# Eight steps of attention ahead of the mask flag instead of six, a set-up in another order with multiplied constants, and the mask words split between two engines, in a fused attention and expert kernel on one Trainium2 core

## The chip, the cores and the metric

The kernel runs on one core of one Trainium2 chip. The metric is the device time of one execution in microseconds. All times inside the execution are counted from the start of the profile's span.

## What is computed

The reference is one block of a network on 2048 rows of 256 numbers: gated cross attention on a context of 1601 keys, then a gated mixture of 8 experts, of which each row takes 2. All is float32. Cut to what matters here:

```python
def _layernorm(x, axis=-1, eps=1e-05):
    m = jnp.mean(x, axis=axis, keepdims=True)
    v = jnp.var(x, axis=axis, keepdims=True)
    return (x - m) / jnp.sqrt(v + eps)

# attention: x (1, 2048, 256), context (1, 1601, 256), 16 heads of 64
q = (inputs_q @ Wq).reshape(b, -1, H, HD)
k = (inputs_kv @ Wk).reshape(b, -1, H, HD)
v = (inputs_kv @ Wv).reshape(b, -1, H, HD)
scores = jnp.einsum('bthd,bThd->bhtT', q, k) * (1.0 / jnp.sqrt(HD))
scores = jnp.where(mask, scores, jnp.finfo(jnp.float32).min)
attn = jax.nn.softmax(scores, axis=-1)
out = jnp.einsum('bhtT,bThd->bthd', attn, v).reshape(b, t, H * HD)
return out @ Wo

x = x + jnp.tanh(g_xattn[0]) * attention(_layernorm(x), ctx_1024, mask, Wq, Wk, Wv, Wo)
x = x + jnp.tanh(g_ffn[0]) * experts(_layernorm(x), Wg, W1, W2, W3)
```

The mask is true for the keys past a drawn length, the same for every row. So attention looks at the masked columns alone.

## The kernel before

All engines run programs written out by hand, each in its own fixed order, with semaphores between them. Nothing is scheduled by a planner: what stands first in an engine's code runs first, and a waiting instruction holds up everything behind it on its engine.

**The flag and two branches.** With the given mask, only the last block of 401 keys (columns 1200 to 1600) matters. The kernel does not take this for granted. It loads the whole mask in four pieces and tests it: a reduction over the words of columns 0 to 1199 must give zero (`mask_words` on ScalarE, which writes a throw-away copy into `blocksT` and keeps the accumulated sum in `word_max`), and the words of the last columns are looked at by `mask_words` on VectorE. `mask_flag` combines both on VectorE, TensorE sums the result over the partitions with a 1 x 1 matmul (L1488), and `flag_everywhere` puts `plainflag` where every engine reads it. Each engine then branches: `fast_attention` goes on with the last block only, `full_attention` does all keys. Until the flag is known, only the first `PRE` = 6 steps may run, since they are right in either case.

**A step.** Attention is 128 steps ("duos") of one row tile of 128 rows and one pair of heads. Four steps make a chunk (one pair of heads, 512 rows). Step n runs through the engines like this:

- TensorE: `scores(n)`, eight passes of K=64 (a float32 matmul is two passes) into two of the banks `ps_s`; it waits for `mask_and_max(n - 2)`. Then, in steps 2 to 9, one eighth of the values (`values`, L1432, each waits for ScalarE's copy of the one before), in the steps that `K_STEPS` names one pair of keys (`keys`, L1352), in steps n % 4 == 1 the queries of the next chunk (`queries`, L1359), from step 12 on, every fourth step, probabilities times values (`probs_v`, L1467), and from step 18 on the output projection (L1477), which waits for the newest copy of the queries.
- VectorE: `inverses(n - 1)`, `mask_and_max(n)` (two instructions of L1132, each reads a score bank and gives a row minimum), then a reduction over mask words in the first steps, and `transpose_blocks(n - 2)` (L1144).
- ScalarE: copies out of PSUM (`values`, `keys`, `queries`), `exps(n)` (two exponentials, L732), in the first steps `mask_words`, and a share of the DMAs that regroup `blocksT` into `probsT`.
- GpSimd: in the first four steps the biases out of the mask bytes (L540), and `scale(n - 1)` (L603).
- SyncE: after the flag, 12 regroup DMAs for each chunk.

**Work tied to PRE.** The first 512 rows are normalised in the set-up (L920 to L933). The other 12 tiles are done by VectorE inside the steps, and their places are counted from `PRE`: the statistics of three tiles in each of the steps PRE to PRE + 3 (L920), the means and an inverse square root by Newton steps in step PRE + 4 (L925 and L906 to L914), two tiles normalised in each of the steps PRE + 5 to PRE + 10 (L933). TensorE transposes them from step 20 on.

**Set-up.** SyncE issues the loads in this order: the first 512 rows of x, the last block of the context, the first half of Wk, the first half of Wq, the first quarter of the mask, Wv, the rest of the mask, the second half of Wk, the rest of x, the second half of Wq, and small things. TensorE waits for the constants and for context and Wk, then does `keys(0)` and `keys(1)`, the transposes of the normalised x (L1370), `queries(0)`, and enters step 0.

After attention come routing and the 36 tiles of expert work, which the change does not touch.

## Time and profile before

| | us |
|---|---|
| median of 3 runs | 621.73 |
| lowest, highest | 621.47, 621.78 |
| the profiled execution's own time | 621.88 |
| its span, first to last instruction | 620.1 |
| TensorE busy | 588.6 (95% of the span) |
| VectorE busy | 404.3 (65%) |
| ScalarE busy | 272.3 (44%) |
| GpSimd busy | 309.0 (50%) |
| granted TensorE clock, mean | 0.995 |

The profile is of one execution. "PE" is TensorE's matmuls, "PEld" its weight loads, "DVE" VectorE, "ACT" ScalarE, "POOL" GpSimd, "SPq" and "ACTq" the DMA-issuing side of SyncE and ScalarE. A row of the timeline gives start, duration, engine, line, operation, output and inputs, the count of instructions merged into it, and in brackets how long the engine had been idle before it and what ended that. TensorE's ends are modelled: the start of the next row is the better measure of how long a group occupied it.

### The profile page before, as it was taken

Reading aid. Unit: us, or ns where it says so; the run is one execution under the profiler, and the core shown is the slowest. Engines: PE = TensorE matmul, PEld = TensorE weight load, DVE = VectorE, ACT = ScalarE, POOL = GpSimd, SP = SyncE. Lnnn points to the kernel's source line nnn. Section 1 sums busy time; section 2 is a strip of 40 time slices with the busy share of each in tenths; the row PEclk is TensorE's granted clock in tenths of the full one; section 3 lists DMA queues with packets and bytes.
Section 4 is the critical chain, followed back from the end, with each engine's and each line's share of the span. In section 5 each row is a group of like instructions: output and inputs, shape, how many; then the busy total and the mean of one; then the engine's idle time right before and its main releaser. Section 6 shows DMA issues by size and latency. Waiting matters only on the chain.

```text
span 620.1 us, 10909 instructions
## 1 busy us (share of the span) xinstructions
PE 588.6 (95%) x2882; PEld 342.4 (55%) x2883; DVE 404.3 (65%) x1266; ACT 272.3 (44%) x713; POOL 309.0 (50%) x272
## 2 busy tenths in 40 slices
PE   4899999999999999999999999999999999999992
PEld 2444465555546555556555565556665666566661
DVE  3578978898997989988899986266352332223220
ACT  2765665556555655655656564222322112211220
POOL 3643554565564698564796564512573222222221
PEclk9999999999999999999999999999999999999997
DMA  8944576587776789777688676999676443333321
GB/s 317 328 112 105 117 157 166 126 182 151 164 161 163 172 186 212 146 157 191 145 206 179 145 168 141 287 332 297 135 156 122 67 60 53 49 42 49 53 27 22
DMA packets 113971, 93.74 MB, mean 151 GB/s; under 512 B 38512, under 2 KB 107504, under 8 KB 113904
## 3 DMA queue, kind: packets, MB, share of 16 engines
q1 hardware_dynamic: 91824, 70.37, 46.9%
q10 hardware_dynamic: 15360, 13.64, 10.0%
q0 software_dynamic: 6720, 8.95, 8.8%
q8 instruction: 28, 0.46, 0.3%
q14 instruction: 39, 0.32, 0.2%
HBM read 27.72 MB, written 12.36 MB: 65 GB/s over the span
## 4 chain that ended last, share of the span: by engine, by line
PE 71%; DVE 14%; issue 5%; DMA 5%; ACT 4%; ACTq 1%; POOL 0%; SPq 0%; POOLq 0%; DVEq 0%
PE ps_s L1648 17%; PE ps_o L1467 13%; PE ps_s L1419 9%; PE ps_o L1676 8%; PE ps_a L1477 6%; DVE blocksT L1144 5%; DVE probs L1132 4%; DMA out_dram<-yg,ids 4%; PE ps_t L1359 4%; PE ps_o L1432 2%; PE ps_t L1669 2%; ACT probs L732 2%; PE ps_a L1359 2%; PE ps_t L1419 2%; PE ps_t L1352 1%
## 5 line engine op out<-in xcount | busy, mean ns | idle before, releaser
L603 POOL TENSOR_TENSOR probs<-probs,inv_sum 128x802 f32<-128x802 f32 x128 | 195.3, 1526 | 138.2 <-DVE inv_sum L1121 137.1
L732 ACT ACTIVATE probs<-probs,neg_max 128x401 f32<-128x401 f32 x256 | 159.3, 624 | 106.5 <-DVE neg_max L1132 99.0
L1648 PE MATMUL ps_s<-w_sb,xgT 128*128 x288 | 135.4, 593 | 1.5 <-DVE xgT L1150 1.5
L1132 DVE CUSTOM_DVE_ANT_0 probs<-ps_s,biases 128x401 f32<-128x401 f32 x215 | 116.1, 571 | 21.7 <-PE ps_s L1419 20.6
L1144 DVE STREAM_TRANSPOSE blocksT<-probs 128x832 f32<-128x832 f32 x124 | 129.0, 1040 | 0.3 <-POOL probs L603 0.3
L650 POOL DMA_INDIRECT out_dram<-yg,ids x36 | 56.1, 1558 | 144.2 <-DVE yg L1301 107.6
L1467 PE MATMUL ps_o<-probsT,v_sb 128*64 128x512 f32 x496 | 113.3, 598 | 0.0
L1419 PE MATMUL ps_s<-kT,qT 64*128 64x201 f32 (+1 forms) x860 | 108.2, 346 | 3.5 <-DVE neg_max L1132 2.8
L1419 PEld LDWEIGHTS ps_s<-kT,qT 64*128 64x128 f32 x860 | 83.8, 186 | 44.1 <-issue 27.2
L866 ACT COPY gatedT<-ps_t 128x512 f32<-128x512 f32 x36 | 21.1, 586 | 150.8 <-PE ps_t L1669 146.3
L1291 DVE TENSOR_TENSOR gated<-ps_s,silu 128x512 f32<-128x512 f32 x36 | 24.9, 691 | 94.3 <-PE ps_s L1648 82.0
L1648 PEld LDWEIGHTS ps_s<-w_sb,xgT 128*128 128x128 f32 x288 | 51.7, 190 | 38.9 <-issue 37.3
L1676 PE MATMUL ps_o<-w_sb,gatedT 128*128 x288 | 68.1, 379 | 0.8 <-ACT gatedT L866 0.8
L1676 PEld LDWEIGHTS ps_o<-w_sb,gatedT 128*128 128x128 f32 x288 | 54.6, 190 | 23.3 <-issue 17.7
L1467 PEld LDWEIGHTS ps_o<-probsT,v_sb 128*64 128x64 f32 x496 | 32.8, 136 | 60.8 <-issue 60.8
L1477 PE MATMUL ps_a<-wo_sb,oT 128*128 128x256 f32 x240 | 59.7, 391 | 0.4 <-ACT qT L696 0.4
L1477 PEld LDWEIGHTS ps_a<-wo_sb,oT 128*128 128x128 f32 x240 | 43.1, 189 | 12.4 <-issue 7.0
L732 ACT ACTIVATION_READ_ACCUMULATOR probs<-probs,neg_max 128x1 f32 x256 | 48.0, 188 | 0.0
L1359 PE MATMUL ps_t<-xnT,wq_sb 128*128 128x512 f32 x96 | 45.1, 592 | 0.0
L1301 DVE TENSOR_SCALAR yg<-ps_o,xw 128x256 f32<-128x256 f32 x36 | 17.4, 484 | 33.1 <-PE ps_o L1676 32.2
L1121 DVE RECIPROCAL inv_sum<-sum_exp 128x2 f32<-128x2 f32 x128 | 20.5, 161 | 25.4 <-ACT probs L732 25.1
L1419 PE MATMUL ps_t<-kT,qT 64*128 64x200 f32 (+1 forms) x164 | 36.8, 344 | 0.0
(172 smaller groups left out, 515.2 us busy)
## 6 DMA issues: line engine op xcount, KB each, us to landing
probsT<-blocksT SPq DMA_DIRECT2D x276, 96.0 KB
probsT<-blocksT SPq DMA_DIRECT2D x92, 128.0 KB
probsT<-blocksT ACTq DMA_DIRECT2D x96, 96.0 KB
xg_blocks<-x_regrouped SPq DMA_DIRECT2D x156, 32.0 KB
probsT<-blocksT ACTq DMA_DIRECT2D x32, 128.0 KB
w_sb<-W1T_dram SPq DMA_DIRECT2D x8, 512.0 KB, 5.1
w_sb<-W2T_dram SPq DMA_DIRECT2D x8, 512.0 KB, 6.0
w_sb<-W3T_dram SPq DMA_DIRECT2D x8, 512.0 KB, 7.2
```

What stands on the lines that cost most here:

```text
L603: pool.tensor_tensor(duo, duo, inv_sum[:, u:u + 2].unsqueeze(2).to_broadcast([P, 2, LASTK]), ALU.mult)\
L650: pool.indirect_dma_start(out=out, out_offset=bass.IndirectOffsetOnAxis(ap=ids[:, slot:slot + 1], axis=0), in_=yg[:, buf, :], in_offset=No ...
L732: act.activation(probs[:, b, 0:LASTK], probs[:, b, 0:LASTK], ACT.Exp, bias=neg_max[:, b:b + 1], scale=-1.0, accum_out=sum_exp[:, b:b + 1]) ...
L1132: dve.tensor_tensor_reduce(probs[:, b, 0:LASTK], scores_bank(u)[:, 0:LASTK], biases[:, tile, :], HD ** -0.5, 3e38, ALU.add, ALU.min, neg_m ...
L1144: dve.transpose(blocksT[:, c % 2, :, :, t * 32:(t + 1) * 32].rearrange("p c u n -> p u c n"), probs[:, u:u + 2, :].rearrange("p u (c n) -> ...
L1291: dve.tensor_tensor(gated[:, :], ps_s[1][:, :], silu[:, :], ALU.mult).then_inc(gated_ready, 1)
L1359: mm = pe.matmul(q_bank(c)[:, :], wq_sb[:, k, p * P:(p + 1) * P], xnT[:, k, i * GQ:(i + 1) * GQ], start=(k == 0), stop=(k == KT - 1))
L1419: mm = pe.matmul(scores_bank(2 * d + odd)[:, k0:k1], qT[h0:h0 + HD, c % 2, t * P:(t + 1) * P], kT[h0:h0 + HD, c % HP, k0:k1], start=True, ...
L1467: mm = pe.matmul(pv_bank(c)[odd * HD:(odd + 1) * HD, :], v_sb[:, s, 2 * (c % HP) + odd, :], probsT[:, c % 2, s, :, odd, :], start=(s == 0) ...
L1477: mm = pe.matmul(wo_bank(g, half)[:, n * D:(n + 1) * D], oT[:, c % 4, t * P:(t + 1) * P], wo_sb[:, c % HP, :], start=(c == 2 * g), stop=(c ...
L1648: mm = pe.matmul(bank[:, :], xgT[:, buf, k, :], w_sb[:, bass.ds(expert, 1), (n * KT + k) * FH:(n * KT + k + 1) * FH].squeeze(1), start=(k ...
L1676: mm = pe.matmul(ps_o[:, 0:D], gatedT[:, k, :], w_sb[:, bass.ds(expert, 1), 2 * KT * FH + k * D:2 * KT * FH + (k + 1) * D].squeeze(1), sta ...
```

## The change

It has five parts.

1. Set-up on TensorE: as soon as the tile of ones is there (GpSimd now fills it first), 16 matmuls of ones by ones into `ps_o`, which nothing reads.
2. A smaller first load: of Wk only the columns of pairs 0 and 1 (256 columns) are loaded before Wq's first half. Pairs 2 and 3 follow it with a semaphore of their own.
3. Another order: `keys(0)`, the transposes, `keys(1)`, `queries(0)`, `keys(2)`, and then step 0. `keys(2)` was in step 0. The copies on ScalarE follow, with the mask words of the first quarter ahead of the copy of the queries. The keys 0 and 1 go to other banks (`ps_s[2]`, `ps_s[3]`), so step 1 waits for the copy of keys 1. Keys 4 and 5 move from steps 7 and 8 to 8 and 9.
4. `PRE` is 8: steps 6 and 7 are ahead of the flag, and all that is counted from `PRE` on VectorE and ScalarE comes two steps later, the regroup DMAs of the first chunk on ScalarE too (steps 8 and 9). The flag's 1 x 1 matmul uses `ps_t[0]` and waits for the third copy of keys.
5. Mask words: quarter 0 by ScalarE in the set-up, quarter 1 by a new VectorE reduction in step 0, quarters 2 and 3 by ScalarE in steps 1 and 4. VectorE's words of the last columns come in steps 0, 1 and 3.

The core of the diff:

```diff
+WARM = 16
+WORDS_DVE = (1,)
+WORDS_ACT = {1: 2, 4: 3}
+WORDS_LAST = {0: 1, 1: 2, 3: 3}
-PRE = 6
-K_STEPS = {0: 2, 6: 3, 7: 4, 8: 5, 10: 6, 12: 7}
+PRE = 8
+K_STEPS = {6: 3, 8: 4, 9: 5, 10: 6, 12: 7}
...
             load_x(0)
             sp.dma_start(ctx_last[:, :, 0:LASTK], ctxT[:, LAST0:].rearrange("(k p) n -> p k n", p=P)).then_inc(kv_in, 16)
-            load_half(wk_sb, Wk, 0, kv_in)
-            load_half(wq_sb, Wq, 0, w_in[0])
+            load_part(wk_sb, Wk, 0, 2, kv_in)
+            load_part(wq_sb, Wq, 0, 4, w_in[0])
+            load_part(wk_sb, Wk, 2, 4, wk0_in)
...
+            pool.memset(ones[:, :], 1.0).then_inc(const_ready, 1)
             pool.memset(mask8[:, :, SKP - 4:], 0).then_inc(mask_pad, 1)
...
-                if n + 1 < MASK_DMAS:
-                    mask_words(n + 1)
-                if n % 4 in (2, 3) and 0 <= (n - 6) // 4 < CHUNKS - 1:
+                if n in WORDS_ACT:
+                    mask_words(WORDS_ACT[n])
+                if n % 4 in (2, 3) and 1 <= (n - 6) // 4 < CHUNKS - 1 or n in (PRE, PRE + 1):
...
             keys(0)
-            keys(1)
             move_xnT(0)
             move_xnT(1)
+            keys(1)
+            mask_words(0)
             queries(0)
-            mask_words(0)
+            keys(2)
             for n in range(PRE):
                 step_of(n)
...
+                if c in WORDS_DVE:
+
+                    dve.tensor_reduce(word_max[:, 0, c:c + 1], words[:, :, 0:LAST0 // 4], AX.XY, ALU.max)\
+                       .then_inc(words_of, 1)
...
         def _(pe):
+            pe.wait_ge(const_ready, 1)
+            for n in range(WARM):
+
+                pe.matmul(ps_o[:, 0:P], ones[:, :], ones[:, :], start=True, stop=True)
             pe.wait_ge(const_ready, CONSTS)
             pe.wait_ge(kv_in, CTX_WK)
...
                 if n == PRE - 1:
                     pe.wait_ge(flag_step, 5)
-                    pe.matmul(ps_t[1][0:1, 0:1], ones[:, 0:1], rowflag[:, 0:1], start=True, stop=True).then_inc(flag_sum, 1)
+                    pe.wait_ge(k_ready, 3)
+                    pe.matmul(ps_t[0][0:1, 0:1], ones[:, 0:1], rowflag[:, 0:1], start=True, stop=True).then_inc(flag_sum, 1)
...
             keys(0)
-            keys(1)
             transpose_xn(0)
             transpose_xn(1)
+            keys(1)
             pe.wait_ge(w_in[0], 16)
             pe.wait_ge(xnT_ready, 2)
             queries(0)
+            pe.wait_ge(wk0_in, 16)
+            keys(2)
```

**ScalarE, from its first copy to step 4.** Here `kT<-ps_s` is a copy of keys, `xnT` and `qT` copies of the transposed x and of the queries, `blocksT,word_max<-mask` the mask words, `v_sb` a copy of values, `probs` the exponentials of a step. Before:

```order
L692 ACTIVATE kT<-ps_s 128x401 x2
L700 COPY xnT<-ps_t 128x512 x2
L696 COPY qT<-ps_a 128x512
L708 ACTIVATE blocksT,word_max<-mask 128x1200
L732 ACTIVATE probs,sum_exp<-probs,neg_max 128x401 x2
L708 ACTIVATE blocksT,word_max<-mask 128x1200
L692 ACTIVATE kT<-ps_t 128x401
L732 ACTIVATE probs,sum_exp<-probs,neg_max 128x401 x2
L708 ACTIVATE blocksT,word_max<-mask 128x1200
L696 COPY qT<-ps_a 128x512
L732 ACTIVATE probs,sum_exp<-probs,neg_max 128x401 x2
L708 ACTIVATE blocksT,word_max<-mask 128x1200
```

And in the change (its line numbers):

```order
L709 COPY xnT<-ps_t 128x512 x2
L701 ACTIVATE kT<-ps_s 128x401
L717 ACTIVATE blocksT,word_max<-mask 128x1200
L705 COPY qT<-ps_a 128x512
L701 ACTIVATE kT<-ps_t 128x401
L741 ACTIVATE probs,sum_exp<-probs,neg_max 128x401 x4
L717 ACTIVATE blocksT,word_max<-mask 128x1200
L705 COPY qT<-ps_a 128x512
L741 ACTIVATE probs,sum_exp<-probs,neg_max 128x401 x2
L749 COPY v_sb<-ps_o 128x512
L741 ACTIVATE probs,sum_exp<-probs,neg_max 128x401 x2
L749 COPY v_sb<-ps_o 128x512
```

The mask words left steps 0 and 2. One piece stands in step 1, ahead of the second copy of queries, and the last in step 4, ahead of the third copy of values.

**VectorE, from the flag's second half to the first normalised tiles after it.** `BN_STATS` are the statistics of three tiles (the means and the Newton steps follow them), `ISA probs` and `ISA neg_max` belong to `mask_and_max`. Before, steps 9 and 10:

```order
L1144 STREAM_TRANSPOSE blocksT<-probs 128x2x13x32
L920 BN_STATS halves<-xs 128x6 x3
L1121 RECIPROCAL inv_sum<-sum_exp 128x2
L1132 ISA probs,neg_max<-ps_s,biases 128x401
L1132 ISA neg_max 128x1
L1132 ISA probs,neg_max<-ps_s,biases 128x401
L1132 ISA neg_max 128x1
L1144 STREAM_TRANSPOSE blocksT<-probs 128x2x13x32
L925 BN_AGGR mean_var<-halves 128x2 x12
L906 TENSOR_SCALAR stat<-mean_var 128x12
```

And in the change, steps 11 and 12:

```order
L1160 STREAM_TRANSPOSE blocksT<-probs 128x2x13x32
L931 BN_STATS halves<-xs 128x6 x3
L1137 RECIPROCAL inv_sum<-sum_exp 128x2
L1148 ISA probs,neg_max<-ps_s,biases 128x401
L1148 ISA neg_max 128x1
L1148 ISA probs,neg_max<-ps_s,biases 128x401
L1148 ISA neg_max 128x1
L1160 STREAM_TRANSPOSE blocksT<-probs 128x2x13x32
L936 BN_AGGR mean_var<-halves 128x2 x12
L917 TENSOR_SCALAR stat<-mean_var 128x12
```

The rows are the same ones two steps later: the fourth group of statistics moved from step 9 to step 11, the means and Newton steps from step 10 to step 12, the six pairs of normalised tiles from steps 11 to 16 to steps 13 to 18.

## Rows read from the trace of the kernel before

**Rows 1.** The page's chain that ended last, share of the span by engine

```profile
PE 71%; DVE 14%; issue 5%; DMA 5%; ACT 4%; ACTq 1%; POOL 0%; SPq 0%; POOLq 0%; DVEq 0%
```

**Rows 2.** Windows by stage: length, busy us (count) of PE, PEld, DVE, ACT, POOL; clock, DMA, GB/s

```profile
7.40:32.50 25.10, 22.06 (x80) 10.82 (x81) 13.80 (x48) 15.52 (x37) 13.81 (x9) 1.00 0.95 327
32.50:67.80 35.30, 35.30 (x159) 16.59 (x158) 28.86 (x103) 20.34 (x55) 14.35 (x11) 1.00 0.43 99
67.80:86.00 18.20, 17.23 (x103) 9.04 (x101) 16.05 (x45) 11.81 (x33) 11.58 (x8) 1.00 0.89 183
```

**Rows 3.** Timeline of the set-up, all engines: start, duration, engine, line, operation, idle before

```profile
7.43 5.56 PE L1352 MATMUL ps_s<-ctx_last,wk_sb 128*128 128x401 f32 x8 [7.43 <-DMA wk_sb<-Wk_dram]
...
8.87 1.38 DVE L933 TENSOR_SCALAR xn<-xs,mean_var,stat 128x256 f32<-128x256 f32 x4
...
10.86 0.57 DVE L939 TENSOR_REDUCE word_max<-mask 128x4 f32<-128x404 int32 x1 [0.61 <-DMA mask<-mask_dram]
...
12.83 1.04 PE L1370 MATMUL ps_t<-ident,xn 128*128 128x128 f32 x8
...
14.68 1.95 PE L1359 MATMUL ps_a<-xnT,wq_sb 128*128 128x512 f32 x4 [0.82 <-ACT xnT L700]
...
17.31 0.95 PE L1419 MATMUL ps_s<-kT,qT 64*128 64x201 f32 x8 [0.68 <-ACT qT L696]
...
18.19 1.61 PE L1352 MATMUL ps_t<-ctx_last,wk_sb 128*128 128x401 f32 x4
...
18.42 0.58 DVE L1132 CUSTOM_DVE_ANT_0 probs<-ps_s,biases 128x401 f32<-128x401 f32 x1 [6.98 <-PE ps_s L1419]
```

**Rows 4.** Timeline of steps 0 to 3, ScalarE and what waits for it

```profile
19.04 0.63 ACT L732 ACTIVATE probs<-probs,neg_max 128x401 f32<-128x401 f32 x1 [0.58 <-DVE neg_max L1132]
...
20.28 1.19 ACT L708 ACTIVATE blocksT<-mask 128x1200 f32<-128x1200 int32 x1
...
27.16 0.58 ACT L740 COPY v_sb<-ps_o 128x512 f32<-128x512 f32 x1
...
27.79 1.98 PE L1432 MATMUL ps_o<-wv_sb,ctx_last 128*128 128x512 f32 x4 [1.51 <-ACT v_sb L740]
```

**Rows 5.** Timeline of steps 5 and 10, TensorE

```profile
33.50 1.98 PE L1432 MATMUL ps_o<-wv_sb,ctx_last 128*128 128x512 f32 x4
...
54.28 0.95 PE L1419 MATMUL ps_s<-kT,qT 64*128 64x201 f32 x8
```

**Rows 6.** Timeline of steps 9 to 21, VectorE

```profile
48.36 1.04 DVE L920 BATCH_NORM_STATS2 halves<-xs 128x6 f32<-128x256 f32 x3
49.31 0.15 DVE L1121 RECIPROCAL inv_sum<-sum_exp 128x2 f32<-128x2 f32 x1
...
52.60 0.87 DVE L925 BATCH_NORM_AGGREGATE mean_var<-halves 128x2 f32<-128x6 f32 x12
...
55.88 0.58 DVE L1132 CUSTOM_DVE_ANT_0 probs<-ps_s,biases 128x401 f32<-128x401 f32 x1
...
57.84 0.69 DVE L933 TENSOR_SCALAR xn_late<-xs,mean_var,stat 128x256 f32<-128x256 f32 x2
58.45 0.16 DVE L1121 RECIPROCAL inv_sum<-sum_exp 128x2 f32<-128x2 f32 x1
...
64.38 0.58 DVE L1132 CUSTOM_DVE_ANT_0 probs<-ps_s,biases 128x401 f32<-128x401 f32 x1 [0.51 <-PE ps_s L1419]
...
74.52 0.58 DVE L1132 CUSTOM_DVE_ANT_0 probs<-ps_s,biases 128x401 f32<-128x401 f32 x1
...
86.08 0.58 DVE L1132 CUSTOM_DVE_ANT_0 probs<-ps_s,biases 128x401 f32<-128x401 f32 x1 [1.91 <-PE ps_s L1419]
```

**Rows 7.** Timeline, DMA issue on SyncE's queue, the first chunk's regroup

```profile
35.72 7.87 SPq L361 DMA_DIRECT2D probsT<-blocksT  x12
```

**Rows 8.** Timeline of steps 16 to 18, TensorE

```profile
68.39 0.95 PE L1419 MATMUL ps_s<-kT,qT 64*128 64x201 f32 x8 [0.58 <-DVE neg_max L1132]
...
77.00 1.99 PE L1477 MATMUL ps_a<-wo_sb,oT 128*128 128x256 f32 x8 [0.40 <-ACT qT L696]
```

More of the change, by code:

```diff
@@ L212, in build @@
         wo_in = sem("wo_in")
-        kv_in, wk1_in, wv_in = sem("kv_in"), sem("wk1_in"), sem("wv_in")
+        kv_in, wk0_in, wk1_in, wv_in = sem("kv_in"), sem("wk0_in"), sem("wk1_in"), sem("wv_in")
         mask_in = [sem(f"mask{c}_in") for c in range(MASK_DMAS)]
         mask_pad, biases_ready = sem("mask_pad"), sem("biases_ready")
-        words_seen, mask_seen = sem("words_seen"), sem("mask_seen")
+        words_seen, words_of, mask_seen = sem("words_seen"), sem("words_of"), sem("mask_seen")
         const_ready, pads_ready = sem("const_ready"), sem("pads_ready")
@@ L307, in settled @@
             eng.wait_ge(w_in[1], 16)
+            eng.wait_ge(wk0_in, 16)
             eng.wait_ge(wk1_in, 16)
@@ L312, in settled @@
             eng.wait_ge(pads_set, 2)
-            eng.wait_ge(k_ready, 3)
+            eng.wait_ge(k_ready, 4)
             eng.wait_ge(xnT_ready, 2)
             eng.wait_ge(biases_ready, MASK_DMAS)
-            eng.wait_ge(words_seen, MASK_DMAS)
+            eng.wait_ge(words_seen, MASK_DMAS - len(WORDS_DVE))
+            eng.wait_ge(words_of, len(WORDS_DVE))
             eng.wait_ge(mask_seen, MASK_DMAS)
-            eng.wait_ge(q_ready, 2)
+            eng.wait_ge(q_ready, 3)
             eng.wait_ge(v_ps, PRE - 2)
@@ L374, in load_x, with load_part @@
                   .then_inc(x_in[g], 16)
-            def load_half(w_tile, w, half, done):
-                c0, c1 = half * H * HD // 2, (half + 1) * H * HD // 2
+            def load_part(w_tile, w, c0, c1, done):
+                c0, c1 = c0 * P, c1 * P
                 sp.dma_start(w_tile[:, :, c0:c1], w[:, c0:c1].rearrange("(k p) n -> p k n", p=P)).then_inc(done, 16)
@@ L392, in _ @@
                 load_mask(c)
-            load_half(wk_sb, Wk, 1, wk1_in)
+            load_part(wk_sb, Wk, 4, 8, wk1_in)
             for g in range(1, NR):
                 load_x(g)
-            load_half(wq_sb, Wq, 1, w_in[1])
+            load_part(wq_sb, Wq, 4, 8, w_in[1])
             sp.dma_start(gates[:, 0:1], g_xattn.partition_broadcast(P)).then_inc(g_in, 16)
@@ L525, in _ @@
             pool.memset(used_rows[:, :], 0.0).then_inc(pads_ready, 1)
-            pool.memset(ones[:, :], 1.0).then_inc(const_ready, 1)
             pool.memset(pads[:, :], 0.0).then_inc(pads_made, 1)
@@ L609, in step_of @@
                 if n == PRE - 1:
-                    pool.wait_ge(words_seen, MASK_DMAS)
+                    pool.wait_ge(words_seen, MASK_DMAS - len(WORDS_DVE))
+                    pool.wait_ge(words_of, len(WORDS_DVE))
                     pool.wait_ge(mask_seen, MASK_DMAS)
@@ L705, in mask_words @@
                 if c >= 1:
-                    act.wait_ge(words_seen, c)
+                    act.wait_ge(words_seen, len([b for b in range(c) if b not in WORDS_DVE]))
                 words = mask8[:, c * MT:(c + 1) * MT, :].bitcast(I32)
@@ L792, in step_of @@
                         act.wait_ge(pv_ready, c - 1)
-                    for g in (0, 1) if n % 4 == 2 else (2, 3):
+                    for g in (0, 1) if n % 2 == 0 else (2, 3):
                         for b in (2, 3) if c == CHUNKS - 2 else (3,):
@@ L949, in mask_flag @@
                 dve.wait_ge(mask_seen, MASK_DMAS)
-                dve.wait_ge(words_seen, MASK_DMAS)
+                dve.wait_ge(words_seen, MASK_DMAS - len(WORDS_DVE))
+                dve.wait_ge(words_of, len(WORDS_DVE))
                 dve.tensor_reduce(rowflag[:, 0:1], word_max[:, 0, 0:MASK_DMAS], AX.X, ALU.max).then_inc(flag_step, 1)
@@ L1198, in step_of @@
                     mask_and_max(n)
-                if n + 1 < MASK_DMAS:
-                    mask_words(n + 1)
+                if n in WORDS_LAST:
+                    mask_words(WORDS_LAST[n])
                 if 2 <= n < LAST_DUO + 2:
@@ L1351, in keys @@
                 for k in range(KT):
-                    mm = pe.matmul((ps_s[p] if p < 2 else ps_t[p % 2])[:, 0:LASTK], wk_sb[:, k, p * P:(p + 1) * P],
+                    mm = pe.matmul((ps_s[2 + p] if p < 2 else ps_t[p % 2])[:, 0:LASTK], wk_sb[:, k, p * P:(p + 1) * P],
                                    ctx_last[:, k, 0:LASTK], start=(k == 0), stop=(k == KT - 1))
@@ L1410, in scores @@
                     if c < HP:
-                        pe.wait_ge(k_ready, max(2, c + 1))
+                        pe.wait_ge(k_ready, c + 1)
+                if d == 1:
+                    pe.wait_ge(k_ready, 2)
                 if d == BURST + 2:
```

8 lines of the change are left out of this document (4 added, 4 removed).

## The prediction

> **What bounds the kernel now.** I read the page's chain first. It is PE for 71% of the span and DVE for 14% [rows 1], so TensorE's own work sets the end nearly everywhere, and the question for each saved microsecond is whether VectorE can follow. The windows by stage say where the slack is [rows 2]. From 7.4 to 32.5 us PE is busy for 22.06 of 25.10 us. From 32.5 to 67.8 it is busy throughout. From 67.8 to 86 it loses 1.0 us, and there DVE is busy for 16.05 of 18.20. So the change can gain in the first 33 us, and the gain must pass a stretch in which VectorE is nearly full.
>
> The set-up [rows 3]: PE starts at 7.43, when context and Wk have landed, and its eight first passes run at half pace: 5.56 us for eight against 1.61 for four later on. The granted clock reads 1.00 in the window all the same, so I go by the durations: the first passes are at 1.2 GHz, the later at 2.4. The normalised x is ready at 8.87 + 1.38 = 10.25 us, but PE is not free for its transposes before 12.83.
>
> The early steps [rows 4]: the words of the mask (1.19 us each) stand on ScalarE ahead of the copies that PE waits for. The copy of the first values starts at 27.16, and PE waits 1.51 us for it.
>
> The stretch behind [rows 6, 8]: in step 10 VectorE spends 52.60 to 55.88 on aggregates, Newton steps and an inverse, and from there it has no idle time but 0.51 us at 64.38 and a few tenths, until it waits 1.91 us for PE in step 21. In it PE waits 0.58 and 0.40 us.
>
> **Set-up, term by term.** The transposes no longer wait for both keys. One pair of keys is over before 10.25, whatever its pace: even from 7.43 its four passes take half of 5.56 us, to 10.2. So the smaller first load buys nothing by itself, its end is covered by the wait for x. I cost the extra DMA issue at nothing: SyncE issues ahead of the data, and the first mask quarter is used at 10.86 at the earliest, while ScalarE now reaches it at about 13.3.
>
> From 10.3 on, at full pace: transposes 0.9 (to 11.2), keys 1 1.5 (to 12.7, beside it ScalarE's two copies of x), queries 0 1.8 (to 14.5), keys 2 1.45 (to 15.9), from the rows of 1.04, 1.61 and 1.95 us, whose last tenths overlap the next row. The mask words run on ScalarE from 13.3 to 14.6, beside the queries. So scores(0) starts at 15.9 instead of 17.31. Keys 2 also left step 0, so scores(1) starts at 16.8.
>
> The multiplied constants: 16 matmuls are 32 passes of 128 columns. The transposes, eight in 1.04 us, are such passes at full pace, so at half pace each takes some 0.21. From about 1.1 us (the tile of ones) all 32 would end at 7.9 at the latest; if the clock rises as after the first pass before (half pace until 12.2, 4.8 us), they end near 7.0. Keys 0 then end between 8.4 and 10.6, so between nothing and 0.3 us late. I take nothing. The Trainium skill, TensorE: Matmul & The Clock Gate, Part 1, says that the moment of the rise varies from run to run; no row here can show that, and by it the sum would be the 0.3 us at most.
>
> **Steps 0 to 5: a chain through three engines.** VectorE's first maximum starts 1.1 us after scores(0) [rows 3], at 17.0, and its two instructions take 1.0. Behind them now stand the last words (0.5) and the new reduction over 1200 words. No row has that size. The nearest is 404 words in 0.57 us [rows 3]; an instruction on two columns takes 0.15 [rows 6], so 0.42 goes by the word, and 1200 words take about 1.3 to 1.4; the bounds are 1.2 (ScalarE's pass over the same words) and 1.7 (0.57 x 3). I take 1.3, being the same instruction. With the inverse (0.1) the maximum of step 1 starts at 19.9, where its scores are there at 17.8. ScalarE follows 0.6 behind (18.42 to 19.04): exponentials of step 1 from 20.5 to 21.7 (a pair takes 20.28 - 19.04 = 1.24), mask words to 22.9, queries' copy 0.5, exponentials of step 2 to 24.7, copy of values 0. PE goes on 0.63 after that copy's start, as 27.16 to 27.79, at 25.3: 2.5 us earlier than 27.79. Then scores(4) 1.9 later at 27.2, its maximum 28.2, exponentials 28.8 to 30.05, and the last mask words, now in step 4, to 31.25. The third copy of values waits for them, and PE starts values 3 at 31.9 instead of 33.50 [rows 5]. 0.9 of the 2.5 us is given back by these moved words.
>
> From there PE has no idle time up to step 10, before and after: the same groups in another order, and the flag's matmul (0.1). Values 3 to scores(10) took 54.28 - 33.50 = 20.8, so scores(10) starts at 52.8: **1.5 us earlier**. The branch comes at step 8 now; before it cost PE nothing (no idle in [rows 2]), and values of 1.9 us still cover the flag's way.
>
> **Steps 10 to 18: what VectorE carries.** All its work on the other 12 tiles moved two steps later, away from steps 6 and 7, in which it waits for PE anyway, and toward this stretch. The maximum of step 10 starts at 52.8 + 1.0 = 53.8 (before 55.88, since the Newton steps stood ahead of it). From that of step 10 to that of step 17 it took 74.52 - 55.88 = 18.6 us [rows 6]. Of this, one pair of normalised tiles falls out, since its step is 18 now: -0.61. The waits for PE fall out: -0.6. The fourth statistics come in: 49.31 - 48.36 = +0.95. The aggregates and Newton steps come in: 55.88 - 52.60 less the inverse of 0.12, +3.16. Together 21.5, so the maximum of step 17 starts at 75.3, **0.8 us later** than 74.52. ScalarE's exponentials of step 17 and the queries' copy follow it, and the output projection of step 18 waits for that copy [rows 8]: 77.0 becomes 77.8. PE would reach scores(16) 1.5 us earlier and the projection too; so it stops there for about 1.8 and 1.3 us, where it lost 0.58 and 0.40.
>
> Behind it VectorE has the last pair of tiles more, 0.61, which fits into its 1.91 us of waiting in step 21. From there both kernels do the same, and PE's lag of 0.8 us stays to the end.
>
> **The sum.** -1.5 up to step 10, +2.3 in steps 10 to 18, = +0.8 us. Against the profiled execution's own time, 621.88, this is 622.7. That execution lies 0.15 above the median of the three runs, so in the median I expect 621.73 + 0.8 = 622.5. About 0.2% (1.24 us) is what a measurement of this kernel tells from no change; the forecast lies inside. Its own range is 621.6 to 623.4: the new reduction at its bounds moves it by -0.1 to +0.4, the set-up by 0.3, and each of the tenths that I rounded by as much again.
>
> **Rivals.**
>
> *The gain of the set-up survives.* The stretch of VectorE is hidden and the 1.5 us reach the end: 620.2. For it: PE loses only 1.0 us in that stretch before, and VectorE's wait of 1.91 us in step 21. Against it: that wait lies behind the output projection, and the stretch is overfull by 2.3 us before it. My sum would have to be wrong by the size of the whole Newton block less a little. 0.18.
>
> *The clock falls back: slower.* Between keys 0 (over at 8.4) and x (10.3) PE now has nothing to do for 1.9 us, straight after it was warmed. If it is at the lower level at 10.3, the passes of the next 4.8 us take twice as long, up to 2.4 us at scores(0), and nothing behind has slack to take it back: 622.5 + 2.4 = 624.9. It decides itself by the duration of the first keys after the transposes: 1.6 us or 2.7 for four passes. Against it: before, an idle time of 1.51 us is followed by four passes of 512 columns in 1.98 us, full pace [rows 4]. The Trainium skill, same page and part, states that an idle tensor engine goes back to the half rate. By that rule the multiplied constants are lost if the gap is long enough, and the time is this rival's. 0.10.
>
> *The first regroup comes too late: slower.* Its DMAs on SyncE wait for the flag, now in step 7 at about 39.9, and take 7.87 us to issue [rows 7]; ScalarE's last two are issued after the exponentials of step 9, at about 51. VectorE's transposes of step 10 wait for them at 54.8. If they landed over 3.5 us after issue, VectorE would stand still at the start of its full stretch, and all that it loses arrives at the end: 1 to 2 us, 624. 0.08.
>
> *The change does not do what it says*, because something I have not seen holds the order of the first steps: the time stays within a few tenths of 621.7, or moves a little to either side. 0.04.
>
> **How the numbers follow.** Forecast 0.60 (0.54 inside the 0.2%, 0.06 slower), the gain survives 0.18 (0.15 faster, 0.03 inside), clock 0.10 slower, regroup 0.08 (0.07 slower, 0.01 inside), the rest 0.04 (half faster, half slower). Faster 0.17, same 0.58, slower 0.25. The range takes in the first rival and the regroup, and leaves out the clock: 620.2 to 624.2.
>
> **What would show it.** Right: transposes at 10.3 instead of 12.83; scores(0) at about 15.9; values 1 at 25.3, values 3 at 31.9, scores(10) at 52.8; PE waits of some 1.8 and 1.3 us before scores(16) and the first output projection, named as VectorE's row minimum and ScalarE's copy of queries; the projection at 77.8. Wrong: PE waits in steps 14 to 18 no longer than 0.6 us (the first rival), four key passes of over 2.5 us after the transposes (the clock), an idle VectorE before the transposes of step 10 with a DMA as its cause (the regroup).

## The result and the profile after the change

| | before | the change |
|---|---|---|
| median, us | 622.17 | 624.71 |
| lowest, highest | 621.47, 623.15 | 622.10, 628.84 |
| runs | 18 | 18 |
| the profiled execution's own time | 621.88 | 623.68 |
| its span | 620.1 | 621.9 |
| its mean granted clock | 0.995 | 0.991 |

The change is 0.43% slower: the ratio is 1.0043, with a 95% interval of 1.0033 to 1.0052, or 2.5 us. The forecast was 622.5 and "within 0.2%", in a range that ended at 624.2. So the change cost more than was forecast, and its time lies outside the range. The spread is new too: 1.7 us between the lowest and the highest before, 6.7 us with the change. Two single executions of the experiments, of 1560.08 and 3061.02 us, are left out of every number below.

TensorE's timeline of the change, set-up and steps 0 to 5 (columns as in the rows ahead of the prediction):

```profile
1.03 6.45 PE L1364 MATMUL ps_o<-ones 128*128 128x128 f32 x32 [1.03 <-POOL ones L524]
7.32 1.51 PE L1372 MATMUL ps_s<-ctx_last,wk_sb 128*128 128x401 f32 x4
10.37 1.09 PE L1390 MATMUL ps_t<-ident,xn 128*128 128x128 f32 x8 [1.53 <-DVE xn L944]
11.29 1.51 PE L1372 MATMUL ps_s<-ctx_last,wk_sb 128*128 128x401 f32 x4
...
15.80 1.63 PE L1442 MATMUL ps_s<-kT,qT 64*128 64x201 f32 x16
...
25.12 1.98 PE L1455 MATMUL ps_o<-wv_sb,ctx_last 128*128 128x512 f32 x4 [2.10 <-ACT v_sb L749]
...
31.68 1.98 PE L1455 MATMUL ps_o<-wv_sb,ctx_last 128*128 128x512 f32 x4 [0.90 <-ACT v_sb L749]
```

These answer to [rows 3 to 5]. The keys of pair 0, four passes, need 1.51 us at full pace where the eight passes of pairs 0 and 1 took 5.56. The transposes start at 10.37 instead of 12.83, scores(0) at 15.80 instead of 17.31, values 1 at 25.12 instead of 27.79. The wait in front of values 1 grew from 1.51 to 2.10 us.

The same engine in steps 16 to 18, where the last two rows answer to [rows 8]:

```profile
68.58 0.95 PE L1442 MATMUL ps_s<-kT,qT 64*128 64x201 f32 x8 [1.77 <-DVE neg_max L1148]
69.46 3.65 PE L1490 MATMUL ps_o<-probsT,v_sb 128*64 128x512 f32 x16
73.04 0.95 PE L1442 MATMUL ps_s<-kT,qT 64*128 64x201 f32 x8
...
77.70 1.99 PE L1500 MATMUL ps_a<-wo_sb,oT 128*128 128x256 f32 x8 [0.91 <-ACT qT L705]
```

VectorE, the new reduction and the two ends of its full stretch [rows 6]:

```profile
18.39 1.39 DVE L954 TENSOR_REDUCE word_max<-mask 128x1 f32<-128x1200 int32 x1
...
53.89 0.58 DVE L1148 CUSTOM_DVE_ANT_0 probs<-ps_s,biases 128x401 f32<-128x401 f32 x1 [2.90 <-PE ps_s L1442]
...
75.25 0.56 DVE L1148 CUSTOM_DVE_ANT_0 probs<-ps_s,biases 128x401 f32<-128x401 f32 x1
...
86.77 0.58 DVE L1148 CUSTOM_DVE_ANT_0 probs<-ps_s,biases 128x401 f32<-128x401 f32 x1 [1.44 <-PE ps_s L1442]
```

And the windows of the change: two of the stretches of [rows 2], then a late one that no row above shows. The number behind the five busy times is the granted clock.

```profile
32.50:67.80 35.30, 33.96 (x149) 15.43 (x147) 25.74 (x96) 18.56 (x49) 14.19 (x10) 1.00 0.43 98
67.80:86.00 18.20, 16.51 (x94) 8.58 (x96) 17.11 (x51) 11.15 (x33) 10.98 (x8) 1.00 0.86 177
357.00:371.70 14.70, 13.02 (x94) 9.11 (x96) 11.72 (x33) 8.87 (x25) 9.71 (x9) 1.00 0.83 182
371.80:375.20 3.40, 3.40 (x12) 1.00 (x10) 3.30 (x15) 1.33 (x4) 1.22 (x2) 0.50 0.46 77
```

VectorE is busy for 17.11 of 18.20 us in the full stretch, where it was for 16.05. The last line is a stretch at half the clock, 1.2 GHz, for 3.4 us. In this execution everything in front of it follows the predicted schedule. At 357 us the change is 0.67 us behind (TensorE's L1402 at 357.31, before its L1382 at 356.64). Behind the slow stretch TensorE's next group that had to wait starts at 384.62 before and at 386.70 with the change, 2.1 us later:

```profile
384.62 0.39 PE L1401 MATMUL ps_o<-counts,ones 128*128 128x40 f32 x2 [0.68 <-ACT oT L747]
```

```profile
386.70 0.39 PE L1421 MATMUL ps_o<-counts,ones 128*128 128x40 f32 x2 [0.45 <-ACT oT L756]
```

TensorE's last group is 2.1 us later too (609.42 against 607.28). The spans differ by only 1.8 us, because GpSimd's last transfer waits 4.50 us for the one before it, where it waited 4.88. So the difference is 0.7 us of schedule and 1.4 of this stretch, which the profiled execution of before did not have, less 0.3 at the very end.

The mean clock of an execution needs one more word. Every profile also shows half clock in its last 6 to 8 us, when TensorE has nothing left to do (before: from 613.5 us, its last group starts at 607.28). This alone makes the 0.995 of before, and a difference of 0.001 between two runs can be the length of that end.

The change's own runs say that one such stretch does not make the median. Their mean clocks go down in steps, and the times go up with them: 622.10 at 0.995; seven runs of 623.4 to 623.9 at 0.991 or 0.992; four of 624.6 to 625.4 at 0.988 or 0.989; four of 625.7 to 626.0 at 0.986 or 0.987; and 627.62 and 628.84 at 0.985 and 0.980. One stretch of 3.4 us at half the clock lowers the mean by 0.5 x 3.4 / 622, which is 0.0027, about one of these steps.

### The profile page after: what moved, and what is told of

Read it like the earlier page. It is cut to its first block, busy times and chain, and to the rows that moved or that the text cites. A ratio compares the mean times of both kernels' runs of the same rounds, so it can differ in the third digit from the quotient of the medians.

```text
span 621.9 us, 10974 instructions
## 1 busy us (share of the span) xinstructions
PE 594.0 (96%) x2914; PEld 347.7 (56%) x2915; DVE 404.9 (65%) x1267; ACT 271.2 (44%) x711; POOL 308.5 (50%) x272
## 4 chain that ended last, share of the span: by engine, by line
PE 68%; DVE 17%; issue 6%; ACT 4%; DMA 3%; another core or an unknown queue 1%; ACTq 1%; POOL 0%; DVEq 0%; POOLq 0%
PE ps_s L1674 19%; PE ps_o L1490 12%; PE ps_o L1702 9%; PE ps_s L1442 8%; DVE blocksT L1160 6%; PE ps_a L1500 5%; DVE probs L1148 5%; PE ps_t L1379 4%; PE ps_t L1695 2%; ACT probs L741 2%; DMA out_dram<-yg,ids 2%; PE ps_t L1442 2%; PE ps_o L1455 2%; PE ps_a L1379 1%; PE ps_a L1410 1%
## 5 line engine op out<-in xcount | busy, mean ns | idle before, releaser
L1490 PE MATMUL ps_o<-probsT,v_sb 128*64 128x512 f32 x496 | 114.7, 605 | 0.0
L1317 DVE TENSOR_SCALAR yg<-ps_o,xw 128x256 f32<-128x256 f32 x36 | 17.4, 484 | 32.8 <-PE ps_o L1702 31.9
```

The costliest lines, as they stand in the source:

```text
L1490: mm = pe.matmul(pv_bank(c)[odd * HD:(odd + 1) * HD, :], v_sb[:, s, 2 * (c % HP) + odd, :], probsT[:, c % 2, s, :, odd, :], start=(s == 0) ...
```

## The theories

**A**: the schedule costs 0.7 us as predicted; the rest is the clock, which falls behind waits of TensorE that are longer than any in the early part of before (1.51 us [rows 4] against 2.10, 1.77 and the 1.5 to 1.9 in front of the transposes). **A1**, a variant, puts it on the multiplied constants: TensorE warmed early is let down later. **B**: the waits in the schedule alone cost the 2.5 us, through buffers and transfers, and the clock is incidental. The expectations below were written before their runs.

The chips differ: on the three of the experiments, the kernel before had medians of 620.79, 622.49 and 620.91 us. Every ratio is against it on the same chip.

## Experiments

### The first four: what belongs to which part

**The kernel before once more** (no edit).

> The kernel before once more, unchanged, to see the mean granted clock of each of its executions, which the runs shown so far give for the change alone (there 0.995 in one of 18 executions, 0.991 in seven, 0.980 to 0.989 in ten). Theory A (extra drops of the clock are bound to how the change starts TensorE or to how its program lies in time): nearly all executions at 0.995, at most one in five lower, 621.5 to 622.3 us. Rival B (the drops come in any kernel with these routing stages, and the change had bad luck): as many executions at 0.991 and below as the change has, spread 622 to 626.

Measured: 620.71 (12 runs), ratio 0.9998 (0.9989 to 1.0008). Its clocks were 0.994 in three runs, 0.992 in four and 0.991 in five, with means of 620.1, 620.6 and 621.4 us. So before has slow stretches as well, where I had taken its 0.995 for normal: about one in an execution, on this chip in nine of twelve. This is neither what theory A expected (nearly all at 0.995) nor its rival (a spread like the change's). This profile has one stretch, from 369.7 us. What the change adds must be stretches beyond this one.

**No multiplied constants.**

```diff
-WARM = 16
+WARM = 0
```

> The change without its 16 matmuls of ones (WARM = 0). By my sum of the set-up, keys 0 run at half pace to about 9.4 and the transposes and the first of keys 1 too: scores(0) 1.0 to 1.6 us later than 15.8, and that much at the end if the clock does nothing else: 623.5. Theory A1 (the multiplied constants fix where the clock's drops fall, or draw them): the drops of the change vanish, all executions at 0.994 or 0.995, 622.8 to 623.8 with little spread. Rival A2 (the drops belong to the rest of the change): clocks of 0.980 to 0.991 as in the change, 624.5 to 629.

Measured: 624.04 (6 runs), ratio 1.0043 (1.0027 to 1.0060), clocks 0.989 to 0.992, where theory A1 expected 0.994 or 0.995 and A2 0.980 to 0.991.

```profile
8.80 3.01 PE L1372 MATMUL ps_s<-ctx_last,wk_sb 128*128 128x401 f32 x4 [8.80 <-DMA wk_sb<-Wk_dram]
18.44 1.63 PE L1442 MATMUL ps_s<-kT,qT 64*128 64x201 f32 x16
...
27.76 3.36 PE L1455 MATMUL ps_o<-wv_sb,ctx_last 128*128 128x512 f32 x4 [2.10 <-ACT v_sb L749]
31.05 1.22 PE L1442 MATMUL ps_s<-kT,qT 64*128 64x201 f32 x8
```

TensorE's timeline without the constants: the first keys run at half pace, scores(0) comes 2.6 us later than in the change. Here stands the first early slow stretch in a profile: four passes of values took 3.36 us instead of 1.98, right behind the 2.10 us. It came without any warmed start, so A1 falls as the whole explanation. With or without the constants the ratio is the same within its interval, so in the change as a whole they bring neither a gain nor a loss that these runs can tell.

**The constants alone**, in the kernel before.

```diff
+            pool.memset(ones[:, :], 1.0).then_inc(const_ready, 1)
             pool.memset(mask8[:, :, SKP - 4:], 0).then_inc(mask_pad, 1)
...
+            pe.wait_ge(const_ready, 1)
+            for n in range(16):
+                pe.matmul(ps_o[:, 0:P], ones[:, :], ones[:, :], start=True, stop=True)
             pe.wait_ge(const_ready, CONSTS)
```

> The kernel before with nothing but the 16 matmuls of ones ahead of its first keys. Keys 0 and 1 run at full pace, so TensorE is free for the transposes at 10.3 instead of 12.8, and scores(0) starts some 2 us earlier. By the sum: -1.5 to -2 at scores(0), of which the chain over ScalarE's mask words keeps about 1.5 at step 6, and which VectorE's place in steps 10 to 17 does not eat, as its work there lies where it did: 620.2 without drops. Theory A1: granted clocks of 0.980 to 0.991 in most executions and 621 to 626 us. Rival A2: 0.995 throughout and 620.0 to 620.6.

Measured: 620.15 (12 runs), ratio 0.9983 (0.9973 to 0.9993).

```profile
1.03 5.53 PE L1347 MATMUL ps_o<-ones 128*128 128x128 f32 x32 [1.03 <-POOL ones L516]
7.72 2.93 PE L1355 MATMUL ps_s<-ctx_last,wk_sb 128*128 128x401 f32 x8 [1.16 <-DMA wk_sb<-Wk_dram]
...
15.15 0.95 PE L1422 MATMUL ps_s<-kT,qT 64*128 64x201 f32 x8 [0.68 <-ACT qT L696]
...
25.63 1.98 PE L1435 MATMUL ps_o<-wv_sb,ctx_last 128*128 128x512 f32 x4 [1.50 <-ACT v_sb L740]
```

Eight passes of keys take 2.93 us instead of 5.56, and scores(0) starts at 15.15 where [rows 3] has 17.31. At the output projection 1.6 us of it are left (74.83 against 76.44 in the profile of before on this chip), since VectorE's work lies where it did. This is the part of the change that pays, and alone it is 0.6 us below the kernel before in the median.

It is less than the 1.6 us, and the clock says why. The twelve runs lie at 0.988 to 0.993 with a mean of 0.9903, where before has 0.9923 on this chip, though no wait got longer. The profile has no early stretch, but the one near 370 us is twice as long:

```profile
366.40:373.20 6.80, 6.80 (x32) 5.16 (x33) 4.10 (x15) 2.61 (x9) 1.71 (x2) 0.50 0.57 134
```

TensorE is 1.6 us ahead of the profile of before on this chip until 325 us, and 0.2 us ahead at 389 us. So A1 is right in part: the constants alone came with a lower mean clock. Why, and whether they also lower it in the change, no run separates.

**VectorE's row work early again**, in the change: statistics of six tiles in each of steps 8 and 9, the Newton steps in step 10, as before.

```diff
-                if PRE <= n < PRE + 4:
-                    statistics(GT + 3 * (n - PRE), GT + 3 * (n - PRE) + 3)
-                if n == PRE + 4:
+                if PRE <= n < PRE + 2:
+                    statistics(GT + 6 * (n - PRE), GT + 6 * (n - PRE) + 6)
+                if n == PRE + 2:
                     mean_and_rsqrt(GT, NT, 11)
-                if PRE + 5 <= n < PRE + 11:
-                    for t in (2 * (n - PRE - 5), 2 * (n - PRE - 5) + 1):
+                if PRE + 3 <= n < PRE + 9:
+                    for t in (2 * (n - PRE - 3), 2 * (n - PRE - 3) + 1):
```

> The change with VectorE's work on the 12 late tiles packed closer: statistics of six tiles in each of steps 8 and 9, means and Newton steps in step 10, normalised tiles in steps 11 to 16 as before. Theory (the +2.3 us of steps 10 to 18 come from that work's place): the waits of TensorE before scores(16) (1.77) and before the first output projection (0.91) fall to at most 0.6 and 0.4, the projection starts at about 75.9 instead of 77.7, and the profile is 1.6 to 2.0 us shorter at that point. Rival (they come from the later flag or the regroup): no change. If the drops of the clock come as in the change, the median is 622.5 to 623; without them 620.4.

Measured: 620.85 (12 runs), ratio 1.0005 (0.9994 to 1.0016), clocks 0.988 to 0.992.

```profile
67.24 0.95 PE L1442 MATMUL ps_s<-kT,qT 64*128 64x201 f32 x8 [0.58 <-DVE neg_max L1148]
...
75.84 1.99 PE L1500 MATMUL ps_a<-wo_sb,oT 128*128 128x256 f32 x8 [0.39 <-ACT qT L705]
```

The two waits are back at the 0.58 and 0.40 us of [rows 8], and the output projection starts 1.86 us earlier than in the change. This confirms that the two steps' delay of VectorE's work is what ate the gain. Yet the median is only that of the kernel before, because its clocks were lower than the other's on this chip (means 0.9901 and 0.9923). At 0.992 its runs average 619.8 us, where before at that clock has 621.0.

### The next four: where the clock falls, and filling the waits

**The change once more** (no edit), in twelve executions, and **one profile more**.

> The change once more, unchanged, on one chip with the next two kernels and the kernel before, so that time and mean granted clock can be set side by side. Theory (schedule +0.7 us, and the rest from more time at half clock): executions of equal clock differ from the kernel before by 0.5 to 1.0 us, and the mean clock is 0.002 to 0.005 lower. Rival (the schedule itself costs 2.5 us): executions at 0.994 or 0.995 are 2.5 us above those of before with the same clock.

> The change once more for a second look at where the half clock falls. Theory (a stretch at half clock follows one in which TensorE had idle time of over a microsecond or only very small matmuls): each stretch at half clock that the windows show starts within 4 us behind such a place: the waits at 8.8, 23 and 67 us, the routing matmuls of 8 columns (near 190, 280, 368 us), the change from attention to experts near 402. Rival (it falls anywhere): in the middle of full stretches.

Measured: 624.15 (12 runs, up to 628.68), ratio 1.0030 (1.0011 to 1.0049); the further profiled execution took 624.3. By clock, three runs at 0.995 average 622.03, where before has 621.88 at that clock; two at 0.991 average 623.71 against 622.88. So at equal clock the change costs 0.15 to 0.8 us, which is the schedule. What is left of the 1.7 us between the medians is the lower mean clock, 0.9898 against 0.9925, again the size of one stretch in an execution. The profile of the first fell on an execution with three early stretches. Its windows:

```profile
11.00:14.40 3.40, 3.40 (x10) 2.21 (x9) 0.57 (x1) 1.17 (x2) 1.53 (x1) 0.50 1.03 394
14.40:28.00 13.60, 11.50 (x52) 5.88 (x51) 8.07 (x25) 9.69 (x24) 7.78 (x6) 1.00 1.07 364
28.00:31.40 3.40, 3.40 (x12) 1.44 (x10) 1.12 (x4) 1.05 (x3) 2.71 (x2) 0.50 0.68 205
31.40:72.40 41.00, 38.06 (x168) 17.70 (x170) 30.80 (x110) 23.54 (x61) 16.96 (x11) 1.00 0.39 89
72.40:75.80 3.40, 3.40 (x14) 1.09 (x12) 3.40 (x11) 1.56 (x6) 1.52 (x1) 0.50 1.02 226
```

And its TensorE timeline around them:

```profile
10.49 1.57 PE L1390 MATMUL ps_t<-ident,xn 128*128 128x128 f32 x8 [1.95 <-DVE xn L944]
11.86 2.76 PE L1372 MATMUL ps_s<-ctx_last,wk_sb 128*128 128x401 f32 x4
...
17.61 1.63 PE L1442 MATMUL ps_s<-kT,qT 64*128 64x201 f32 x16
...
26.93 2.75 PE L1455 MATMUL ps_o<-wv_sb,ctx_last 128*128 128x512 f32 x4 [2.10 <-ACT v_sb L749]
29.61 1.71 PE L1442 MATMUL ps_s<-kT,qT 64*128 64x201 f32 x8
...
71.90 1.27 PE L1442 MATMUL ps_s<-kT,qT 64*128 64x201 f32 x8 [1.77 <-DVE neg_max L1148]
73.10 4.98 PE L1490 MATMUL ps_o<-probsT,v_sb 128*64 128x512 f32 x16
78.01 0.95 PE L1442 MATMUL ps_s<-kT,qT 64*128 64x201 f32 x8
...
81.69 1.99 PE L1500 MATMUL ps_a<-wo_sb,oT 128*128 128x256 f32 x8
```

Each stretch at 0.50 begins within 1.1 us of the end of a wait: 0.5 behind the 1.95, 1.1 behind the 2.10, 0.5 behind the 1.77. The starts compare with the profile of the change at 15.80, 25.12 and 73.04: +1.8 us at scores(0), +1.8 at values 1, +5.0 at scores(17). The output projection gives 1.0 of it back, since its own wait of 0.91 is gone, and is 4.0 us late. The kernel is the same, and so are the two waits of 2.10 and 1.77 us; only the clock behind them differs. The further profile had one early stretch, from 68.6 us, again at the wait in front of scores(16). There its TensorE lost 1.6 us at first, but the projection started only 0.6 us late (78.33 against 77.70), since its wait of 0.91 was gone. So a stretch at this place costs some 0.6 us in the end, and one behind the transposes or at values 1 its full 1.3 to 1.7.

**Three waits filled**, in the change. The matmuls of ones write into banks that are free there, and nothing reads them.

```diff
+            def busy(bank, count):
+                for _ in range(count):
+                    pe.matmul(bank[:, 0:P], ones[:, :], ones[:, :], start=True, stop=True)
...
+                if n == 16:
+                    pe.wait_ge(k_ready, 7)
+                    busy(ps_t[0], 7)
...
+                if n == 3:
+                    busy(ps_t[1], 9)
                 if 2 <= n < 2 + 2 * NS:
                     values(n - 2)
...
             keys(0)
+            busy(ps_o, 6)
```

> The change with more matmuls of ones in three places where TensorE waits: 6 ahead of the transposes (wait of 1.5 us), 9 ahead of values 1 (2.1 us), 7 ahead of scores(16) (1.77 us). Each fits into its wait, so the schedule stays as it is, +0.7 us. Theory (the additional half clock of the change comes behind these waits): the mean clock rises to that of the kernel before or above (0.992 or more on a chip where before has that), and the median falls by 1 to 2 us below the change's. Rival 1 (the drops come from the warm-up's own early start or from elsewhere): clock and median as in the change. Rival 2 (more constant work makes the clock worse): lower clock.

Measured: 623.77 (11 runs), ratio 1.0023 (1.0012 to 1.0035). The mean clock is 0.9911, where the change has 0.9898, and none of these runs is below 0.988, where the change had four of twelve. Its profile has one slow stretch only, from 371.8, and the schedule is the change's: output projection at 77.89 behind a wait of 0.91. No run lies above 625.44 us, where the change had four, up to 628.68. But the expected 1 to 2 us in the median did not come: it moved by 0.4 us, and the two ratios' intervals overlap. The change itself therefore does not prove the filling. Three runs are at 0.988; where the second stretch in them lay no profile shows, and the doubled one near 370 us, as with the constants alone, is a candidate.

**VectorE early and two waits filled**: the edit of the fourth experiment, with `busy` in front of the transposes and of values 1. The third wait is 0.58 us there and needs none.

> The packed VectorE work of e1_dve_early, with the first two fillings (its third wait is 0.58 us only). Theory: the schedule's -1.2 us against before and a mean clock like before or better: 1.0 to 1.5 us below the kernel before in the median, 2 to 4 us below the change. Rival (drops stay): as e1_dve_early, level with before.

Measured: 621.09 (8 runs), ratio 0.9973 (0.9963 to 0.9984); the three runs at 0.995 and 0.996 lie between 619.5 and 620.0. It is 1.4 us below before and 3.1 below the change in the medians of this chip.

### The last four: the filling alone, side by side

> The packed VectorE work without fillings again, now on one chip with the filled version. Theory (fillings save half clock, the packing saves schedule): at equal clock as fast as the filled version within 0.3 us, but a mean clock lower by 0.002 to 0.003 and a median 0.8 to 1.5 us higher. Rival (fillings do nothing, the two calls had different chips): same mean clock and median as the filled version.

> The filled version with packed VectorE work once more, on another call. Theory: 1.0 to 1.6 us faster than the kernel before again, mean clock like that of before. Rival: level with before, the first measurement was luck.

> A third look at the change's half clock. Theory: stretches at half clock start only within 4 us behind the waits of TensorE at 8.8, 23 and 67 us, behind the routing matmuls near 190, 280 and 368 us or behind the change to the experts near 402 us.

> A third look at the half clock of the kernel before. Theory: none in the first 100 us (its waits there are 0.8, 0.7, 1.5 and 0.6 us, and the first of them come while the clock has just risen), at most one behind the routing matmuls near 368 us. Rival: half clock in the first 100 us as often as in the change.

The first two kernels differ by the fillings and nothing else. VectorE early, unfilled: 622.04 (11 runs), ratio 1.0011 (0.9999 to 1.0022), mean clock 0.9893, nine of eleven runs at 0.988 or 0.989. Filled: 619.80 (11 runs), ratio 0.9984 (0.9975 to 0.9993), mean clock 0.9917, one of eleven at 0.989. The unfilled kernel's profile:

```profile
11.00:25.50 14.50, 12.40 (x58) 6.65 (x57) 7.95 (x23) 10.07 (x24) 8.62 (x6) 1.00 1.06 375
25.50:28.90 3.40, 3.40 (x6) 1.10 (x6) 1.76 (x5) 1.42 (x5) 3.40 (x3) 0.50 1.09 346
29.00:100.00 71.00, 68.37 (x348) 34.54 (x345) 58.49 (x186) 42.88 (x115) 33.72 (x22) 1.00 0.56 127
...
370.30:373.70 3.40, 3.40 (x20) 2.32 (x20) 2.13 (x7) 1.52 (x5) 1.44 (x1) 0.50 0.77 145
```

The filled one's:

```profile
11.00:25.50 14.50, 14.50 (x77) 8.82 (x76) 7.83 (x23) 9.96 (x24) 8.50 (x6) 1.00 1.06 375
25.50:28.90 3.40, 3.40 (x14) 1.54 (x14) 2.64 (x8) 1.99 (x6) 3.40 (x3) 1.00 1.09 346
...
368.70:372.10 3.40, 3.40 (x18) 2.37 (x18) 2.10 (x6) 1.52 (x5) 1.48 (x1) 0.50 0.72 145
```

and its TensorE at the place of the wait:

```profile
22.18 0.95 PE L1442 MATMUL ps_s<-kT,qT 64*128 64x201 f32 x8
23.07 2.28 PE L1506 MATMUL ps_t<-ones 128*128 128x128 f32 x18
25.24 1.98 PE L1455 MATMUL ps_o<-wv_sb,ctx_last 128*128 128x512 f32 x4
```

With something to do until 25.24, TensorE keeps 2.4 GHz through the window 25.5 to 28.9, in which the row counts fourteen passes (some of them short ones of ones) against six. Values 1 start 0.1 us later for it, and the gain is 2.2 us in the median and 1.6 in the mean (621.55 against 619.92). The mean is the better measure here: the unfilled runs stand in two groups, and the median jumps from one to the other. A mean clock lower by 0.0024 is at most 0.0024 x 620 = 1.5 us. Theory B, in which the waits cost by themselves, falls: the wait is as long as before, only filled.

The two profiled executions lie 2.75 us apart, more than one stretch. TensorE is 1.5 us apart up to 360 us. Another 0.9 comes at 408 us, where the unfilled one waits 0.78 us for VectorE and the filled one does not. One profile of the kernel before has this wait too, so nothing ties it to the early stretch.

The two further profiled executions: the change took 624.9 us, with half clock from 26.4 and, for 6.8 us, from 371.1. The kernel before took 621.0, with half clock in one place before the end:

```profile
13.00:100.00 87.00, 82.56 (x407) 41.28 (x405) 66.84 (x211) 55.97 (x146) 44.24 (x29) 1.00 0.66 168
...
366.00:370.20 4.20, 2.83 (x25) 2.64 (x26) 3.55 (x9) 1.98 (x7) 2.43 (x3) 1.00 0.88 212
370.20:373.60 3.40, 3.40 (x17) 1.71 (x16) 3.09 (x11) 1.41 (x5) 1.21 (x2) 0.51 0.51 122
```

Half clock between the rise in the set-up and 100 us stands in none of the three profiles of the kernel before, in none of the three of filled kernels and not in that of the constants alone (a wait of 1.50 us). Of the seven profiles with the 2.10 us wait unfilled (the change four times, without constants, VectorE early twice) it stands in five.

The same profiles counted by wait, each unfilled: the half clock came behind the 2.10 us in front of values 1 in four of seven, behind the 1.77 us in front of scores(16) in two of five, behind the 1.3 to 2.0 us in front of the transposes in one of six (at 1.95; 1.99 had none), and behind 1.50 us in front of values 1 in none of four. Length alone does not decide: at the same length some executions fall and others do not.

## Why the prediction was wrong

**Set-up: right.** Transposes at 10.3, seen 10.37; scores(0) at 15.9, seen 15.80. The constants ended at 7.5, between the bounds of 7.0 and 7.9, and keys 0 were over well before x was there.

**Steps 0 to 5: right.** The new reduction 1.3, seen 1.39, near the upper of the two values that the word count gave. Values 1 at 25.3, seen 25.12; values 3 at 31.9, seen 31.68; scores(10) at 52.8, seen 52.91 (a small wait of 0.26 in front of values 6 was not foreseen).

**Steps 10 to 18: right.** Maximum of step 17 at 75.3, seen 75.25; waits of "about 1.8 and 1.3 us", seen 1.77 and 0.91; the projection at 77.8, seen 77.70. The fourth experiment undid just this part and got 1.86 us back of the 2.3 that it was priced at.

**The sum of the schedule: right, with some luck.** +0.8 us was forecast; 0.67 stand at 357 us. Both are against one profile of before, in which the eight first passes took 5.56 us. In its two other profiles they took 4.68 and 5.09, and TensorE is 0.4 to 0.6 us ahead of the first up to 325 us; against these the schedule costs 1.1 to 1.3 us.

**What failed** is the sentence behind it: "From there both kernels do the same, and PE's lag of 0.8 us stays to the end". It took every pass at its duration at full clock. The prediction named two longer waits as its own signs, 1.8 and 1.3 us, and its order made a third grow, at values 1, to which it gave no size. It never asked what these waits do to the clock. The clock rival saw the mechanism, but at one place of three, gave it 0.10, and held against it because a wait of 1.51 us was followed by full pace in before [rows 4]. That row is of one execution and of a shorter wait. The runs show 2.1, 1.95 and 1.77 us to be enough in some executions, with 1.3 to 1.7 us lost behind the transposes and at values 1, and some 0.6 at scores(16). In the runs of one chip the mean clock was 0.9898 with the change against 0.9925 before. The rival's size was about right: its 2.4 us became 1.8 at scores(0), since only part of the passes fell into the slow stretch; but the place where it struck most often in the profiles is the wait in front of values 1, in four of those seven. That its 624.9 lies near the median of 624.71 is luck: its own sign, four key passes of over 2.5 us behind the transposes, stands in one of the change's four profiles.

The price should have stood in the sum, times a chance, at each wait that the sum itself made longer, not in a rival at one of them. The Trainium skill, TensorE: Matmul & The Clock Gate, Part 1, says that an idle tensor engine goes back to the half rate. The trace agrees in kind, with the half clock at 11.0, 28.0 and 72.4 us behind the waits. The page does not say how often a wait of about 2 us is enough; here it was in four of seven profiles at 2.10 us.

**The second thing that failed**: the profile of before, at 0.995, was taken for all executions. Before has a slow stretch near 370 us in two of three profiles. This made no difference to the ratio, since the change has it too, but it makes the comparison of the two profiled executions misleading: 1.4 us of it is this common stretch, and the change's own additional ones are absent from its profiled execution.

**Rivals.** "The gain of the set-up survives": no, VectorE carries what was said. "The first regroup comes too late": no, TensorE and VectorE had no wait for a DMA in step 10. "The change does not do what it says": it does.

**What stays open**: where the second stretch in the filled change's slower runs lay; what sets off the stretch near 370 us and doubles it in two profiles, which was not tried (in all kernels 16 passes of 8 columns behind a wait of 1.37 us stand at this place, and in three profiles it begins while they run); why the constants alone came with a lower mean clock; and how the chance grows with the length of the wait. How much of the change's lower clock lies behind its three waits is therefore shown in its profiles and in the filled pair of the VectorE-early version, not in the medians of the change itself.

## What to carry to other kernels

When a change makes an idle time on TensorE longer, as here from 1.5 to 2.1 us, add the price of a stretch at half clock at that place, times a chance; a schedule that sums to nothing is then a loss. Matmuls that nothing reads, placed into two such waits, gave back 1.6 us in the mean here. Look also for a wait shortly behind, which can take part of the loss up. Before a gain in the set-up is forecast, follow it to the next stretch in which another engine is full, and keep the work of that engine where it had its idle time. Compare more than one profiled execution, by their mean clock, before a difference of 0.3% is laid to the schedule.

## What the runs showed of the hardware

- Half-clock stretches in this kernel are 3.4 us long in the windows (two of 6.8 us, both near 370 us), and occur in some executions of the same program on the same chip and not in others: the change's runs lie between 0.980 and 0.995. The early ones cost 1.5 to 1.7 us each on the spot (the steps between the 1.8, 3.3 and 5.0 us of lag at scores(0), queries 2 and scores(17), less 0.1 of a later x); the last of them cost 0.7 at the output projection. The one near 371 us cost 1.4 us, the doubled ones 3.0.
- The clock fell only when the work had gone on for a while behind the wait of 2.10 us: 0.4, 0.5, 1.1 and 1.3 us behind it in four profiles. One fall at the wait of 1.77 us came right at its end. It is to be looked for behind the wait as well as in it.
- In the kernel before too, a slow stretch stands behind 16 small passes and a wait of 1.37 us in two of three profiled executions, though its wait of 1.5 us in step 3 had none in any.
- 32 passes of 128 columns from 1.03 us on take 5.3 to 6.7 us in different executions, so the rise of the clock at the start varies too. The eight first passes of the kernel before took 5.56, 4.68 and 5.09 us.
- The same kernel differs by 1.7 us between two chips, more than half of the effect that was looked for. The profiles show a place where they differ: at the start of the expert work, near 402 us, TensorE waits 1.5 us for VectorE in three of the four profiles from the slower chip (622.49), and in none of the eight from the two others.
